# Indirect writes and routing pieces moved to other steps, own statistics columns for each tile, a store between the loads

## The reference, cut to what matters

```python
x = hidden_states                                        # (4, 512, 256), float32
x = layernorm(x + attention(x, Wq, Wk, Wv, Wo))          # 16 heads on 4 key-value heads, width 128
x = layernorm(x + experts(x, gate_w, w_gate, w_up, w_down))

# attention: o = 0.5 * causal_softmax_attention(rope(q), rope(k), v) + 0.5 * gated_linear_attention(...)
# gated linear: S = S * exp(g_t) + k_t v_t ;  o_t = q_t S     (scan over tokens)

def experts(x):                                          # T = 2048 tokens, E = 8, F = 176, top 2
    weights = softmax(x @ gate_w.T)
    comb = top-2 of weights, other entries 0
    y_e = (silu(x @ w_gate[e]) * (x @ w_up[e])) @ w_down[e]
    return sum_e comb[:, e] * y_e
```

## Time and profile before

| | us |
|---|---|
| three runs | 980.00, 981.12, 983.92 (median 981.12) |
| the profiled execution's own time | 980.99 |
| its span | 979.2 |
| TensorE busy | 928.0 (95%), 5347 matmuls |
| VectorE, ScalarE, GpSimd busy | 654.4 (67%), 661.8 (68%), 636.1 (65%) |
| granted TensorE clock, mean | 0.98 of full speed |
| DMA | 43.20 MB, mean 44 GB/s |

### The profile page before, as it was taken

How to read it: one execution, slowest core, us unless ns; L and a number is a source line. 1 busy time by engine, 2 the same in 40 slices (tenths; PEclk the granted TensorE clock), 3 DMA queues, 4 the chain that set the end, 5 groups by cost and what they waited for, 6 DMA issues and landing times.

```text
span 979.2 us, 18417 instructions
## 1 busy us (share of the span) xinstructions
PE 928.0 (95%) x5347; PEld 718.5 (73%) x5347; DVE 654.4 (67%) x1597; ACT 661.8 (68%) x2139; POOL 636.1 (65%) x609
## 2 busy tenths in 40 slices
PE   7899999999999999999999999999999989989990
PEld 4678777778787878787887877878777766766770
DVE  4777776767676767677676869676887664431274
ACT  6677777777777777777677776777667664543453
POOL 6878675767565657676767667766658881553342
PEclk9999999999999999999999999999999999997995
DMA  7101100000000000900000000010102121332364
GB/s 250 34 17 33 39 1 2 6 12 6 1 0 0 0 1 10 257 6 2 1 1 1 1 7 6 24 39 3 61 1 79 38 85 45 92 107 84 98 180 133
DMA packets 34050, 43.20 MB, mean 44 GB/s; under 512 B 3756, under 2 KB 27950, under 8 KB 33840
## 3 DMA queue, kind: packets, MB, share of 16 engines
q1 hardware_dynamic: 30224, 33.76, 11.8%
q0 software_dynamic: 3744, 8.43, 2.4%
HBM read 25.58 MB, written 18.43 MB: 45 GB/s over the span
## 4 chain that ended last, share of the span: by engine, by line
PE 85%; DVE 4%; ACT 4%; issue 3%; POOL 2%; another core or an unknown queue 1%; DMA 0%; POOLq 0%; DVEq 0%; ACTq 0%
PE OA L590 14%; PE PR L473 12%; PE S L543 11%; PE MS L563 9%; PE S L572 7%; PE S L689 5%; PE OA L552 5%; PE OA L583 4%; PE OA L706 4%; PE PR L519 3%; PE PR L513 3%; PE S L534 1%; PE MS L502 1%; ACT eqk L821 1%; PE MS L594 1%
## 5 line engine op out<-in xcount | busy, mean ns | idle before, releaser
L1496 POOL TENSOR_TENSOR qd<-eqk,eg 128x512 f32<-128x512 f32 x63 | 75.9, 1205 | 163.1 <-issue 157.2
L590 PE MATMUL OA<-wT,V 128*128 128x512 f32 x320 | 150.2, 600 | 0.2 <-DVE wT L1081 0.2
L783 ACT ACTIVATE S<-S,nm 128x128 f32<-128x128 f32 (+3 forms) x256 | 126.8, 495 | 26.8 <-DVE nm L998 22.8
L821 ACT ACTIVATE eqk<-qkv,nmx 128x128 f32<-128x128 f32 x320 | 124.4, 396 | 6.0 <-DVE nmx L1073 5.5
L998 DVE TENSOR_REDUCE nm<-S 128x2 f32<-128x256 f32 (+3 forms) x128 | 102.0, 817 | 29.1 <-PE S L543 23.4
L590 PEld LDWEIGHTS OA<-wT,V 128*128 128x128 f32 x320 | 60.2, 192 | 70.9 <-issue 70.4
L1484 POOL TENSOR_TENSOR eqk<-eqk,rse 128x640 f32<-128x640 f32 x63 | 79.7, 1265 | 49.9 <-DVE rse L1116 25.7
L1032 DVE TENSOR_TENSOR pr<-S,rl 128x256 f32<-128x256 f32 (+3 forms) x128 | 105.5, 824 | 5.0
L1473 POOL TENSOR_TENSOR rp<-qkv,cos 128x640 f32<-128x640 f32 x64 | 99.9, 1560 | 6.4 <-ACT qkv L811 4.9
L1476 POOL TENSOR_TENSOR rp<-rp,rt 128x640 f32<-128x640 f32 x64 | 99.5, 1554 | 5.0
L1473 POOL TENSOR_TENSOR rt<-qkv,sin 128x640 f32<-128x640 f32 x64 | 99.5, 1555 | 0.0
(11 more groups left out here) (173 smaller groups left out, 2506.1 us busy)
## 6 DMA issues: line engine op xcount, KB each, us to landing
qkv<-slot_x SPq DMA_DIRECT2D x46, 129.0 KB
pr<-plane SPq DMA_DIRECT2D x16, 256.0 KB, 3.1
gu_w<-in_wgu SPq DMA_DIRECT2D x8, 352.0 KB, 3.6
slot_x<-zero SPq DMA_DIRECT2D x2, 1290.0 KB, 9.8
stage<-in_wqkv SPq DMA_DIRECT2D x6, 384.0 KB, 3.4
xraw<-in_x_cols SPq DMA_DIRECT2D x16, 128.0 KB, 2.4
acc<-in_x_rows SPq DMA_DIRECT2D x1, 2048.0 KB, 11.1
dn_w<-in_wdn SPq DMA_DIRECT2D x8, 256.0 KB, 4.2
```

The costliest lines, as they stand in the source:

```text
L590: last = pe.matmul(OA[:, :], V[:, j, :], wT[:, j, :], start=(c == 0 and j == 0), stop=(j == c))
L783: nc.scalar.activation(S[:, h, 0:n], S[:, h, 0:n], ACT.Exp, bias=nm[:, h:h + 1], scale=1.0, accum_out=ls[:, h:h + 1]).then_inc(s_exp, 1)
L821: last = nc.scalar.activation(eqk[:, par, h * 128:(h + 1) * 128], qkv[:, c % C, h * 128:(h + 1) * 128], ACT.Exp, bias=nmx[:, h:h + 1], sca ...
```

## The change

Five edits:

1. Three tables move routing pieces on VectorE: the third comparison from "mid" of k = 21 to "late" of k = 20, the slots from "mid" of k = 24 and 25 to "late" of k = 23 and 24, and `tile_experts` of set 0 out of `slot_bases` (k = 23) to "late" of k = 26.
2. `SEND_AT` gives the 24 writes of set 0 to k = 25 to 30 as 4, 4, 6, 0, 4, 6 instead of 4 each.
3. The eight writes of the last batch come one a step, q = 15 to 22, instead of two a step, q = 14 to 17.
4. `mv`, `ve`, `rstd` and `nmr` of the second normalisation have 16 columns, and the wait of `moments2` for `norm2` is gone. `load_rows`, `combine` and `rs2` come one step earlier (36 + t instead of 37 + t), `norm2` comes one tile a step from q = 40, and VectorE normalises the last tile itself.
5. The first store stands ahead of `load_rows(12)`; the last two tiles are stored one by one, so there are six stores instead of five.

```diff
-        mv = [None] + [sb(f"mv{i}", [P128, 4, 2], F32) for i in (1, 2)]
+        mv = [None] + [sb(f"mv{i}", [P128, (0, 4, TILES)[i], 2], F32) for i in (1, 2)]
...
-        nmr = sb("nmr", [P128, TPB], F32)
+        nmr = sb("nmr", [P128, TILES], F32)
...
-        COMPARE_AT = {("late", 9): 0, ("late", 13): 1, ("mid", 21): 2}
+        COMPARE_AT = {("late", 9): 0, ("late", 13): 1, ("late", 20): 2}
...
-        SLOTS_AT = {("mid", 24): 0, ("mid", 25): 1}
-        SEND_AT = {25: (0, 2), 26: (2, 4), 27: (4, 6), 28: (6, 8), 29: (8, 10), 30: (10, 12)}
+        SLOTS_AT, EXPERTS_AT = {("late", 23): 0, ("late", 24): 1}, ("late", 26)
+        SEND_AT = {25: (0, 2), 26: (2, 4), 27: (4, 7), 29: (7, 9), 30: (9, 12)}
...
-                if q >= 38:
-                    load_rows(q - 38)
-            for t in range(NT - 38, TILES):
+                if q >= 37:
+                    load_rows(q - 37)
...
+            for t in range(NT - 37, TILES):
+                if t == 3 * TPB:
+                    sp.wait_ge(s_xo, TPB)
+                    store(0, TPB)
                 load_rows(t)
...
+            for a, b in ((TPB, 2 * TPB), (2 * TPB, 3 * TPB), (3 * TPB, 3 * TPB + 2), (3 * TPB + 2, TILES - 1)):
+                sp.wait_ge(s_xo, b)
+                store(a, b)
+            sp.wait_ge(s_last, 1)
+            store(TILES - 1, TILES)
+            sp.wait_ge(s_out, 16 * 6)
...
-                if q in (42, 43):
-                    for i in ((0, 1) if q % 4 == 2 else (2, 3)):
-                        norm2(0, i)
-            for n in (1, 2, 3):
-                for i in range(TPB):
-                    norm2(n, i)
+                if q >= 40:
+                    norm2(q - 40)
+            for t in range(NT + 2 - 40, TILES - 1):
+                norm2(t)
...
-                if s == 0:
-                    tile_experts(s)
...
-                i = slice(2 * h, 2 * h + 2)
+                i = slice(TPB * n + 2 * h, TPB * n + 2 * h + 2)
                 dve.wait_ge(s_bn[2], 2 * TPB * n + 4 * h + 2)
-                later(dve, s_xo, TPB * n - 2 + 2 * h)
...
-            later_tiles = {37 + t: t for t in range(3 * TPB)}
+            later_tiles = {36 + t: t for t in range(3 * TPB)}
...
             shift2(3, 1)
+            a = acc[:, TILES - 1, BODY]
+            nc.vector.tensor_scalar(a, a, mv[2][:, TILES - 1, 0:1], rstd[2][:, TILES - 1:TILES], ALU.subtract, ALU.mult).then_inc(s_last, 1)
...
                     for t in range(*SEND_AT[k]):
-                        send(t)
+                        for r in range(2):
+                            send(t, r)
...
-            sends = {14: 12, 15: 13, 16: 14, 17: 15}
-            deviations = {36 + 2 * i: (i // 2, i % 2) for i in range(5)}
+            sends = {15 + i: (3 * TPB + i // 2, i % 2) for i in range(2 * TPB)}
+            deviations = {35 + 2 * i: (i // 2, i % 2) for i in range(5)}
...
                 if q in sends:
-                    send(sends[q])
+                    send(*sends[q])
```

More of the change, by code:

```diff
@@ L165, in layer_kernel @@
         st = [None] + [sb(f"st{i}", [P128, 4, 6], F32) for i in (1, 2)]
-        mv = [None] + [sb(f"mv{i}", [P128, 4, 2], F32) for i in (1, 2)]
-        ve = [None] + [sb(f"ve{i}", [P128, 4], F32) for i in (1, 2)]
-        rstd = [None] + [sb(f"rstd{i}", [P128, 4], F32) for i in (1, 2)]
+        mv = [None] + [sb(f"mv{i}", [P128, (0, 4, TILES)[i], 2], F32) for i in (1, 2)]
+        ve = [None] + [sb(f"ve{i}", [P128, (0, 4, TILES)[i]], F32) for i in (1, 2)]
+        rstd = [None] + [sb(f"rstd{i}", [P128, (0, 4, TILES)[i]], F32) for i in (1, 2)]
         lg = sb("lg", [P128, TILES, E], F32)
@@ L263, in layer_kernel @@
         s_mark, s_back, s_bf = sem("s_mark"), sem("s_back"), sem("s_bf")
+        s_last = sem("s_last")
         s_yg = [sem(f"s_yg{i}") for i in range(4)]
@@ L439, in _, with store @@
                 load_slots(q)
-                if q >= 38:
-                    load_rows(q - 38)
-            for t in range(NT - 38, TILES):
-                load_rows(t)
[L444 to L451, removed]
+                if q >= 37:
+                    load_rows(q - 37)
+            ov = out.rearrange("b (t p) n -> p (b t) n", p=P128)
+            def store(a, b):
+                sp.dma_start(ov[:, a:b, :], acc[:, a:b, BODY]).then_inc(s_out, 16)
+            for t in range(NT - 37, TILES):
+                if t == 3 * TPB:
+                    sp.wait_ge(s_xo, TPB)
+                    store(0, TPB)
+                load_rows(t)
+            for a, b in ((TPB, 2 * TPB), (2 * TPB, 3 * TPB), (3 * TPB, 3 * TPB + 2), (3 * TPB + 2, TILES - 1)):
[4 more added lines that the diff above has]
+            sp.wait_ge(s_out, 16 * 6)
         @block.tensor
@@ L917, in y_out, with norm2 @@
                 nc.scalar.copy(yo[:, q % YO, :], OA[:, 0:HID]).then_inc(s_yo, 1)
[L919 to L922, removed]
+            def norm2(t):
+                a = acc[:, t, BODY]
+                act.wait_ge(s_nmr, t // 2 + 1)
+                nc.scalar.activation(a, a, ACT.Identity, bias=nmr[:, t:t + 1], scale=rstd[2][:, t:t + 1]).then_inc(s_xo, 1)
             def wo_high(i):
@@ L1332, in beside @@
                     slots(0, SLOTS_AT[at, k])
+                if (at, k) == EXPERTS_AT:
+                    tile_experts(0)
             def multiply(q):
@@ L1361, in moments2 @@
             def moments2(n, h):
-                i = slice(2 * h, 2 * h + 2)
+                i = slice(TPB * n + 2 * h, TPB * n + 2 * h + 2)
                 dve.wait_ge(s_bn[2], 2 * TPB * n + 4 * h + 2)
-                later(dve, s_xo, TPB * n - 2 + 2 * h)
                 for j in (2 * h, 2 * h + 1):
-                    nc.vector.bn_aggr(mv[2][:, j, :], st[2][:, j, :]).then_inc(s_bn[2], 1)
+                    nc.vector.bn_aggr(mv[2][:, TPB * n + j, :], st[2][:, j, :]).then_inc(s_bn[2], 1)
                 dve.wait_ge(s_bn[2], 2 * TPB * n + 4 * h + 4)
@@ L1449, in _ @@
                         shift2((t - 2) // TPB, ((t - 2) % TPB) // 2)
-            combine(3 * TPB - 1)
-            moments2(2, 1)
             shift2(2, 1)
@@ L1555, in norm1, with send @@
                                         ALU.subtract, ALU.mult).then_inc(s_x1a, 1)
-            def send(t):
+            def send(t, r):
                 s = 0 if t < SETS[0][1] else 1
-                if t == SETS[s][0]:
+                if t == SETS[s][0] and r == 0:
                     pool.wait_ge(s_sl, s + 1)
@@ L1564, in send @@
                     pool.wait_ge(s_x1a, SETS[s][1])
-                for r in range(2):
-                    nc.gpsimd.indirect_dma_start(slot_x[s], bass.IndirectOffsetOnAxis(ap=sloti[:, r, t:t + 1], axis=0),
-                                                 acc[:, t, :], None).then_inc(s_sent[s], 16)
+                nc.gpsimd.indirect_dma_start(slot_x[s], bass.IndirectOffsetOnAxis(ap=sloti[:, r, t:t + 1], axis=0),
+                                             acc[:, t, :], None).then_inc(s_sent[s], 16)
             def send_back(q):
@@ L1576, in rs2 @@
             def rs2(n, h):
-                i = slice(2 * h, 2 * h + 2)
+                i = slice(TPB * n + 2 * h, TPB * n + 2 * h + 2)
                 pool.wait_ge(s_ve[2], 2 * n + h + 1)
-                nc.gpsimd.tensor_tensor(rstd[2][:, i], ve[2][:, i], neghalf[:, i], ALU.pow).then_inc(s_rs[2], 1)
+                nc.gpsimd.tensor_tensor(rstd[2][:, i], ve[2][:, i], neghalf[:, 0:2], ALU.pow).then_inc(s_rs[2], 1)
             for c in range(2):
```

## The result

Before took 980.12 us in the median of five runs (977.59 to 983.92), after 972.46 (972.01 to 973.54). The ratio is 0.9919, with a 95% interval of 0.9896 to 0.9941: 7.9 us faster (5.8 to 10.2). The forecast was 967.4, 13.6 faster. 972.46 lies some 5 us above it: within the whole range of 961 to 977.5, but outside the 963 to 971 that the forecast gave to its own mechanism, and nearer to rival B's 975.5 than to 967.4. The profiled execution of after took 972.46 with a span of 970.6, 8.5 less than the span of before (unrounded).

The account below looks back on a forecast made before the run. TensorE, holding 85% of the span, was taken as the bound, so only its waits and the end could give time back. Terms -1.9 - 2.0 + 0.9 - 8.1 - 2.5 = -13.6 took 981.0 to 967.4 us, range 961 to 977.5.

Parts of the forecast that it names:

- rival B: Expert stage: issues without a pause make releases late at any count per step; the 10.5 us stall stays, 975.5 us, chance 0.19.
- the signs of being wrong: Expert-stage clock below 0.9; TensorE over 2 us late at the weights' turn in k = 21 or 25, or on a slot load.
- Writes of the last batch: Expert stage: one write a step instead of two wins back 10.5 us of stall and loses 2.4, term -8.1 us.
- I take 2.4 lost: Expert stage: sixteen issues are four groups of four, 1.2 each, 4.8 us; ScalarE's idle time covers about half.
- Rival A: Expert stage: late releases came only from the backlog, so only 0.5 us is lost; 965.5 us, chance 0.20.
- C: Rival, expert stage and attention: late releases cost 0.88 us per write, and groups of six suffer too; slower, 989 us, chance 0.06.
- Routing pieces on VectorE: Attention k = 21, 24, 25: accumulator-add waits of 3.72 us go, 1.8 come back, term -1.9 us.
- The short durations: Moved VectorE pieces estimated at 1.4 and 1.2 us, as GpSimd is between its pieces; long ones would make the term +1.1.
- Writes to the slots in attention: Attention: the k = 29 wait and its low clock go, 3.9 us; k = 28 gains a 1.9 wait, term -2.0 us.
- The late slot load: Last attention step: later writes of k = 30 delay SP's first slot load, term +0.9 us.
- I take the middle: Slot load of the last attention step: +0.9 us, between nothing and an upper end of 1.8 us late.
- The end: Behind the expert stage: last plane write 2.3 us sooner, last normalisation 0.55 less, one more store 0.35, term -2.5 us.

Follow-up runs that it names:

- e1: Before with only the last batch's eight slot writes one a step, on a chip without late releases: 970.22 against 970.44 us, ratio 0.9999.
- e11: After with the last batch's writes two a step from step 14, on a chip without late releases: 966.84 us, ratio 0.9967 against before.
- e5: After unchanged, measured again on a chip with late releases: 972.06 us, before 978.42 beside it, ratio 0.9931.
- e7: After with the second normalisations of tiles 5 and 6 behind ScalarE's last copy: 971.53 us, 0.5 below after.
- e6: After with attention's slot writes 2, 4, 4, 4, none, 6, 4 in k = 24 to 30: 971.67 us, 0.4 below after.
- e8: After with the edits of e4, e6 and e7 together, on a chip with late releases: 968.25 us, ratio 0.9891 against before.
- e2: Before with only attention's changes, the routing pieces' and slot writes' new places, on a chip without late releases: 968.42 us, ratio 0.9978.
- e9: Before unchanged, for a second profile, on a chip without late releases: 972.05 us, ratio 1.0011.
- e10: The edit of e1 against before, on another chip without late releases: 970.30 us, ratio 0.9999.
- e3: After with attention and the last batch's writes as in before, so only the end changed: 968.36 us, ratio 0.9980 against before.
- e4: After with the last batch's writes in steps 14, 15, 17, 18, 20, 21, 23, 24, on a chip without late releases: 966.54 us, ratio 0.9961 against before.

## Why the prediction was right, and where it was off

The direction and the main term were right. The size was helped by the width of the range: it has the part between the forecast's own 971 and B's 975.5, for which no mechanism was written down, and the time fell there. One of the signs of being wrong, a slot load that TensorE waits for by more than 2, came as well.

**Writes of the last batch: right in kind, forecast -8.1, too large.** The two traces give -6.1 (stage -6.9, of which 0.9 is the paired normalisations: 116.77 in e1 against 115.90 in e11), the runs less: -7.7 between the medians on A minus the 3.5 to 4.1 that the rest gives on B and D leaves some 4, on C 2 to 3. The 4 and the 2 to 3 are differences between chips: on no chip with late releases was this edit run by itself. Two steps failed. "I take 2.4 lost", half of four groups of four at 1.2, was 4.5: 120.37 in place of 115.90. It lies between my two ends of 0.5 and 10.5: three stalls of 1.8, 2.0 and 0.7. And the 10.5 was taken from one execution as if it were every one. In that execution the clock fell to 0.66, and its mean over the span was 0.980; on C the runs of before lie between 977.0 (clock 0.986) and 982.9 (0.979). That the profiled execution has about the median's time on A (980.99 and 980.12) hid how wide these runs spread. No second trace of before was taken on A or C, so what another execution loses there is not measured. Rival A (a backlog of 0.5 alone) falls with the groups of 4.25 and 4.48. Rivals B and C fall as they were priced: the sixteen issues cost 4.5, not 10.5 or 14.9. Their mechanism, rows of issues without a pause, is supported on A and C, where pauses win back 1.9 and the late `qkv` of k = 27 comes with six writes in that step (after, e5, e7) and not with four (e6, e8). It is not enough by itself: on B 17 issues in a row (e1 and e2) delay nothing, and behind the six writes of k = 30 in after the profile marks no late release. The late release that C foresaw in k = 28 did come, but beside the wait for `qd`, at no cost.

**Routing pieces on VectorE: right, -1.9.** k = 21 took 11.65 (13.41 before), k = 24 8.78 (10.03), k = 25 11.53 (12.67); k = 22 took 14.52 (13.28) and k = 26 13.58 (13.25). Together -2.6; 1.6 came back where 1.8 was forecast, though in k = 22 rather than at the weights' turn of k = 21. The short durations were the right ones; the product of the late half took, by the timeline of VectorE of after,

```profile
732.28 0.33 DVE L1248 TENSOR_TENSOR part<-onehot,slot 128x96 f32<-128x96 f32 x1
```

where the early ones took 1.46 and 0.46. No GpSimd instruction ran beside it. The prediction read the early ones wrong in one point: not only the 1.46 ran beside a GpSimd product. The 0.46 started at 738.55, when GpSimd's `qd` (738.40 to 738.81) was running, and ended 0.20 behind it; the 1.46 ended 0.19 behind the product beside it (726.93 to 728.48). The Trainium skill, SBUF — State Buffer, section "SBUF: two separate sides", says that such a VectorE instruction is locked out only by a GpSimd instruction that reads SBUF, for the whole of it; the trace agrees with all three durations.

**Writes to the slots in attention: -2.0 forecast, -0.3 to -1.5 found.** The wait on `qd` in k = 29 went (15.45 to 11.57) and k = 28 went from 8.78 to 10.77: 2.0 longer, where the text had 1.9. (The waits named there are 1.27 on `qkv` and 0.30 on `qd`, since the late release hides most of the wait for `qd`; it is 1.75 in e2.) k = 30 took 13.38 (13.02 before). That sums to 1.99 - 3.88 + 0.36 = -1.5. But 1.8 of the gain forecast was the low clock behind the old wait, and that is not there in every execution: with a wait of 2.02 in e9 k = 29 took 15.39, with 2.07 in e1 13.73 and with 2.08 in e10 13.75; without the fall the sum is -0.3 (k = 30 took 13.45 in e1 and 13.44 in e10). The stretch of e9 (e10 has 1.00 there):

```profile
780.00:800.00 20.00, 17.98 (x99) 13.35 (x98) 13.48 (x31) 14.32 (x49) 17.99 (x17) 0.91 0.24 77
```

**The late slot load: +0.9 forecast, +2.3 found.** "I take the middle" failed; the upper end of 1.8 was exceeded, and so was the 2 of wait that stood among the signs of being wrong (2.18 here, 2.08 in e5, 2.47 in e11). From the start of k = 31 to the first group it takes 16.25 in after and 16.06 in e11, 13.89 in before and 13.85 in e10. The wait of 2.18 takes the place of the 1.85 for `pr`, so it adds only 0.3; the rest is the clock of 0.91 at 800, 1.8 us of 20, which the text left out of this term.

**The end: -2.5 forecast, -1.6 by the traces, -2.1 (1.1 to 2.9) by e3.** The last write to the plane is issued 1.14 behind its copy's start, in place of 3.07, and the paired normalisations' 0.9 is won; the two last down-projections lose 1.1. The last two are about as forecast (0.6 and 1.0). The first was not: the text had the write at once behind its copy, within 0.2, which would have won 2.7; it won 1.9, since the write is issued 0.77 behind the copy's end, no sooner than its neighbours (0.79 for the one before). From the write's issue to the end of the span nothing is won, 19.0 in both traces: halving the last normalisation saved 0.5, the second store cost 0.4, and VectorE reaches the last shift 0.1 later. The stores of after (page's form: tile, queue, count, KB, us to landing):

```profile
out<-acc SPq DMA_DIRECT2D x1, 256.0 KB, 2.1
out<-acc SPq DMA_DIRECT2D x2, 128.0 KB, 1.8
```

The half store lands 0.3 sooner, and two side by side land in 1.8 in the median, so there is no sign that the second waits for the first. The Trainium skill, DMA: Bandwidth & Descriptors, section "Anatomy of one DMA — SWDGE (gpsimd) path", gives bytes / 436e3 us for the part that grows with the size, by which 128 KB less is 0.3 (an estimate, since the page's figure is for GpSimd's path and these are SP's stores); the trace agrees, and the extra issue eats it.

So the sum was 5 us too good. By the traces: writes 2.0, slot load 1.4, the end 0.9, attention's writes 0.5, the later start 0.8, with VectorE's part 0.7 better. By the runs the share of the writes is larger, about 4. The forecast of faster by more than half a per cent rested on the right term, since only the stall of A is large enough for it: without late releases the rest gives 3.5 to 4.1, about 0.4%. That the result was taken where releases come late was luck: on B or D a forecast of more than half a per cent would have failed.

## What to carry to other kernels

A loss that one trace shows may belong to that chip and that execution; before a term of 10 us is built on it, profile the kernel before a second time, if possible on a second chip, and compare the clock of the profiled run with that of the others. Long rows of indirect writes on GpSimd are worth a trial with pauses: where releases came late the pauses won back 1.9 us of the stage, and where none did they cost 0.4. Where an engine has little slack, as GpSimd in k = 25 to 30, moving its work between steps moved the wait (e6).

## What the runs showed that I had not expected

Releases come late in some places and not in others: 0 or 10.5 us in the stage for the same program. Whether the chip decides it or something else of the session, one session for each chip can't tell.

The clock isn't decided by the wait alone either. Behind the wait of 2.02 to 2.08 us for `qd` it fell in two executions (before on A, e9 on D: 0.91 over 20 us) and stayed at 2.4 GHz in three others with the same instructions up to there (e1 and e3 on B, e10 on D). In k = 30 TensorE waits 1.98 for VectorE's `gc` in after and 1.98 and 1.99 in e4 and e8; behind it the clock stayed up in after and fell in the other two, and in e9 it fell behind 1.71, where it stayed up in before.

And the fastest kernel where releases come late is neither of the two: e8 on C takes 0.9961 of after's time there, 0.9891 of before's.
